# Gated cross-attention and experts on one core: diagonals of the maxima in halves, norms on ScalarE, a reordered second layer

## The reference

```
x = x + tanh(g_xattn[0]) * mha(layernorm(x), ctx)                 # 16 heads of 16, softmax over 128 keys
x = x + tanh(g_ffn[0])   * soft_experts(layernorm(x))             # 8 experts, silu(gate)*up, routing weights
x = x + tanh(g_xattn[1]) * attention(layernorm(x), ctx, mask)     # one head of 256
x = x + tanh(g_ffn[1])   * top1_experts(layernorm(x))             # 8 experts, relu, capacity 256 tokens each
```

## Time and profile before

| What | Value |
|---|---|
| median of 3 runs | 764.35 us (763.16 to 766.68) |
| profiled execution, its time | 764.7 us |
| its span, first to last instruction | 762.9 us |
| mean granted clock of TensorE | 0.921 of full speed |
| busy: TensorE, VectorE, ScalarE, GpSimd | 646.4, 521.0, 331.2, 229.1 us |
| transfers | 94.51 MB, mean 124 GB/s |

### The profile page before, as it was taken

The page is one execution under the profiler, slowest core; times in us unless marked ns, Lnnn a source line. Parts: engine busy times, 40 slices in busy tenths (PEclk is TensorE's granted clock), DMA queues, the critical chain, the costliest instruction groups (busy, mean ns, idle before and its releaser), DMA issues.

```text
span 762.9 us, 12648 instructions
## 1 busy us (share of the span) xinstructions
PE 646.4 (85%) x4564; PEld 546.7 (72%) x4564; DVE 521.0 (68%) x1362; ACT 331.2 (43%) x530; POOL 229.1 (30%) x155
## 2 busy tenths in 40 slices
PE   5978598899899899999799889999966931799995
PEld 4656366787678778778688777898855821799995
DVE  6877987677877866866776647479458883466662
ACT  4434155355356456456355325152523321455641
POOL 2444624566532212221014010010031242255542
PEclk9879779899999999999999999999989955799998
DMA  7303303335442242333243424434221141964700
GB/s 225 121 15 127 125 1 139 125 135 211 180 166 83 85 165 84 137 113 125 83 165 113 162 87 152 132 124 146 83 69 43 61 161 43 318 210 153 242 20 26
DMA packets 43463, 94.51 MB, mean 124 GB/s; under 512 B 3519, under 2 KB 24383, under 8 KB 42384
## 3 DMA queue, kind: packets, MB, share of 16 engines
q1 hardware_dynamic: 41344, 87.62, 33.6%
q0 software_dynamic: 2064, 6.16, 2.3%
HBM read 72.94 MB, written 21.04 MB: 123 GB/s over the span
## 4 chain that ended last, share of the span: by engine, by line
PE 65%; DVE 24%; issue 5%; ACT 2%; DMA 1%; POOL 1%; DVEq 0%; SPq 0%; ACTq 0%; POOLq 0%
PE psum L1591 43%; PE psum L2097 6%; PE psum L1668 2%; PE psum L1698 2%; PE psum L1628 2%; PE psum L1662 2%; DVE work L1063 1%; DVE scratch L266 1%; DVE x_all L1079 1%; PE psum L1635 1%; PE psum L1647 1%; DVE work L951 1%; PE psum L1962 1%; PE psum L1893 1%; PE psum L1945 1%
## 5 line engine op out<-in xcount | busy, mean ns | idle before, releaser
L1591 PE MATMUL psum<-arena 128*128 128x256 f32 (+1 forms) x2544 | 446.0, 334 | 33.8 <-DVE x_all L1079 15.6
L1591 PEld LDWEIGHTS psum<-arena 128*128 128x128 f32 x2544 | 384.5, 199 | 78.4 <-DVE x_all L1079 14.8
L2135 POOL TENSOR_TENSOR diag<-neg_ident,work 128x1024 fp32r<-128x1024 f32 x32 | 60.9, 1904 | 249.3 <-DVE work L1010 242.5
L1063 DVE TENSOR_TENSOR work<-work,psum 128x512 f32<-128x512 f32 x64 | 43.9, 686 | 62.1 <-PE psum L1591 57.3
L625 ACT ACTIVATE arena<-work 128x512 fp32r<-128x512 f32 x64 | 40.3, 630 | 90.7 <-DVE work L1063 78.7
L1079 DVE SCALAR_TENSOR_TENSOR x_all<-psum,w_exp,x_all 128x256 f32<-128x256 f32 x128 | 55.9, 479 | 27.7 <-PE psum L1591 26.9
L618 ACT ACTIVATE work<-psum 128x512 f32<-128x512 f32 x64 | 38.2, 597 | 56.8 <-PE psum L1591 56.3
L1068 DVE TENSOR_TENSOR arena<-work,arena 128x512 fp32r<-128x512 f32 x64 | 51.8, 810 | 8.7 <-ACT arena L625 8.2
L2218 POOL TENSOR_TENSOR arena<-work,arena 128x1024 fp32r<-128x1024 f32 x4 | 9.5, 2370 | 151.1 <-ACT arena L641 151.1
L1010 DVE TENSOR_REDUCE work<-psum 128x8 f32<-128x1024 f32 x32 | 39.0, 1220 | 15.7 <-PE psum L1647 15.6
L593 ACT ACTIVATE work<-psum 128x1024 f32<-128x1024 f32 x32 | 32.8, 1026 | 35.4 <-PE psum L1668 32.3
(11 more groups left out here) (194 smaller groups left out, 844.8 us busy)
## 6 DMA issues: line engine op xcount, KB each, us to landing
arena<-kept SPq DMA_DIRECT2D x24, 1024.0 KB, 5.6
work<-in_w SPq DMA_DIRECT2D x16, 1024.0 KB
kept<-arena SPq DMA_DIRECT2D x8, 1536.0 KB, 6.1
arena<-kept SPq DMA_DIRECT2D x24, 512.0 KB, 4.8
work<-in_w SPq DMA_DIRECT2D x8, 768.0 KB, 7.8
slots<-fill POOLq DMA_DIRECT2D x1, 2080.0 KB
work<-in_ctxT SPq DMA_DIRECT2D x8, 256.0 KB, 3.0
work<-in_ctxT SPq DMA_DIRECT2D x4, 512.0 KB, 5.2
```

The lines of the kernel that those rows point to most:

```text
L1063: dve.tensor_tensor(gu[i % 2], gu[i % 2], ps[:, UP, :], ALU.mult).then_inc(hm, 1)
L1591: mm = pe.matmul(dst, left(i, k), right(j, k), start=(n == 0), stop=(n == 3 * K2 - 1))
L2135: pool.tensor_tensor(diag, neg_ident[:, :].rearrange("p (o q) -> p o q", o=1).to_broadcast([P, 8, P]), mx[u % 2].rearrange("p (h o) -> p h ...
```

## The change

It has these parts.

- **Diagonals.** GpSimd writes the eight diagonals in two instructions of four heads, each with its own increment of `dg`; the first of the two products of `shift` waits for the first half only.
- **Routing weights.** `expert_weights` no longer divides the two best weights by their own sum, since all weights are divided by their sum afterwards; one clamp goes and the last two multiplies are one.
- **Norms of layer 1.** `normalise_a` and `normalise_b` are now Identity activations of ScalarE with a scale and a shift; VectorE writes the shift (one instruction) behind each root. `root_b` writes its root and shift where the row for the slots carries them, so that `row_numbers` goes.
- **Values.** The bias of the values is added to x by GpSimd (`value_bias`, 16 additions of 128x256) after the norm has read it; `v1_evict` is a copy by ScalarE.
- **Row numbers** come from constants for all groups; the count of a group's experts stands behind `dest`.
- **Order of turn3**, on all engines: group ga+1's moments and root stand first, its transposes and keys are made inside the turn, queries stand before values, and `scores1(ga)` before `xb_transpose(gb)`.
- **Filler products** (`keep_warm`): bf16 128x512 products into a bank that nobody reads, 2, 22, 5, 2 and 4 in the last turn, 5, 2 and 4 in the one before, 44 before the slots.
- **First expert of the slots**: both its low parts are made by VectorE (`first_split`), the second one after all dispatches have landed; GpSimd does no split before its last dispatches.
- **Slots.** The first load is of two tiles, then two, then twelve. All but the first pair of norms are made by ScalarE, after the fourth Relu of a half turn.
- **The end.** The last `down4` signals its first tile by itself and puts the second tile into the other bank; the addition and store of the first tile follow at once. `scatter` waits for each tile by itself.

```diff
 def expert_weights(g):
-    divide_by_sum(7)
     seq(dve.tensor_tensor(r[7], r[7], over_e(rs[1]), ALU.mult))
     seq(dve.tensor_tensor(rt[4], rt[4], rt[7], ALU.add))
-    divide_by_sum(4)
+    seq(dve.tensor_reduce(rs[2], r[4], AX.X, ALU.add))
+    seq(dve.reciprocal(rs[2], rs[2]))
...
-    dve.tensor_scalar(w_exp[g % 2], r[4], tgate[:, 2:3], None, ALU.mult).then_inc(s_wexp, 1)
+    dve.scalar_tensor_tensor(w_exp[g % 2], r[4], tgate[:, 2:3], over_e(rs[2]), ALU.mult, ALU.mult).then_inc(s_wexp, 1)
 def shift(u):
-    pe.wait_ge(dg, u + 1)
     for j in range(2):
+        pe.wait_ge(dg, 2 * u + j + 1)
         mm = pe.matmul(ps[:, ST + j, :], ones_r[:, :], diag[:, 4 * j:4 * j + 4, :], ...
 def diagonals(u):
...
-    pool.tensor_tensor(diag, neg_ident..., mx[u % 2]..., ALU.mult).then_inc(dg, 1)
+    for j in range(2):
+        sel = slice(4 * j, 4 * j + 4)
+        pool.tensor_tensor(diag[:, sel, :], neg_ident..., mx[u % 2][:, sel]..., ALU.mult).then_inc(dg, 1)
+def normalise_b(g):                                  # ScalarE; normalise_a alike
+    act.wait_ge(sb_ok, g + 1)
...
+        act.activation(xn_b[t % GB], x_all[:, t, 0:D], ACT.Identity, bias=x_all[:, t, D + 1:D + 2],
+                       scale=x_all[:, t, D:D + 1]).then_inc(nb, 1)
 def turn3(ga, gb):                                   # VectorE
+    if more:
+        stats_a(ga + 1, 0); moments_a(ga + 1, 0); root_a(ga + 1, 1)
     attention_gates(gb)
-    if ga is not None:
-        xa_low(ga)
     add_attention(gb)
     moments_b(gb)
-    root_b(); normalise_b(gb)
-    if ga is not None:
-        v1_add(ga)
-    row_numbers(gb)
-    xb_low(gb)
+    root_b(gb)
     if ga is not None:
         mask_and_max(ga)
-    if ga is not None and ga + 1 < G:
-        stats_a(ga + 1, 0); moments_a(ga + 1, 0); root_a(ga + 1, 1); normalise_a(ga + 1)
+    xb_low(gb)
+    if ga is None:
+        first_split(0, w4_l1.sem)
     pick_expert(gb)
-    count_experts(gb)
+    slot_and_gate(gb)
     pick_place(gb)
+    if more:
+        xa_low(ga + 1)
 def turn3(ga, gb):                                   # TensorE
     probs_transpose(gb)
-    if ga is not None:
-        xa_transpose(ga)
+    if last: keep_warm(2)
     attend(gb)
-    if ga is not None:
-        k1_project(ga); v1_project(ga); q1_project(ga)
+    if last: keep_warm(22)
+    else: q1_project(ga); v1_project(ga); scores1(ga)
     xb_transpose(gb)
-    if ga is not None:
-        scores1(ga)
+    if more: xa_transpose(ga + 1)
+    else: keep_warm(5)
     logits1(gb)
+    if not more: keep_warm(2)
     logits1_transpose(gb)
+    if more: k1_project(ga + 1)
+    else: keep_warm(4)
     places(gb)
+xa_transpose(2); k1_project(2)
 turn3(2, 1); turn3(3, 2); turn3(None, 3)
+keep_warm(44)
 def turn3(ga, gb):                                   # ScalarE
     probs_copy(gb)
     if ga is None:
-        split(0, 0, 0)
+        split(0, 0, 0); split(0, 0, 1)
     else:
-        xa_high(ga); k1_evict(ga); q1_evict(ga)
+        q1_evict(ga)
+        if more: normalise_a(ga + 1)
+        v1_evict(ga)
+    normalise_b(gb)
     xb_high(gb)
...
     gate_exp(gb)
+    if more: xa_high(ga + 1); k1_evict(ga + 1)
 # GpSimd, after the weights of layer 1
 ctx_low(0)
+value_bias(0); value_bias(1); ctx_low(1); value_bias(2)
 pool.wait_ge(s_disp, 16)
-ctx_low(1); ctx_low(2); dispatch(0); ctx_low(3); dispatch(1); dispatch(2); split_w1(0, 0); dispatch(3)
+ctx_low(2); dispatch(0); value_bias(3); ctx_low(3); dispatch(1); dispatch(2); dispatch(3)
 for f in range(8):                                   # ScalarE, turn of the slots' experts
     hidden(g, i, f)
     if more and f == 1:
         split(*nxt, 0)
+    if more and f == 3:
+        act.wait_ge(s_xs[1 + i], 16)
+        slots_norm(*nxt)
```

More of the change, by code:

```diff
@@ L335, in block_kernel @@
         oh1, loc1, dest = sem("onehot_ready"), sem("places_ready"), sem("rows_ready")
-        s_xs = [sem("first_slots_loaded"), sem("other_slots_loaded")]
+        s_xs = [sem(f"{n}_slots_loaded") for n in ("first", "second", "other")]
         s_raw4 = [sem(f"expert1_weights_loaded{i}") for i in range(2)]
@@ L634, in zone_exps, with normalise_a @@
                 act.activation(rt[5], rt[3], ACT.Exp, scale=-1.0 / 0.3).then_inc(r_out, 1)
+            def normalise_a(g):
+                act.wait_ge(sa, g + 1)
+                if g:
+                    act.wait_ge(nat, GB * g)
+                else:
+                    act.wait_ge(x1t, B)
+                for t in range(g * GB, (g + 1) * GB):
+                    act.activation(xn_a[t % GB], x_all[:, t, 0:D], ACT.Identity, bias=shiftA[:, t:t + 1], scale=rstdA[:, t:t + 1]
+                                   ).then_inc(na, 1)
             def ctx3_high(g):
@@ L841, in _ @@
             silu(31, 1)
+            normalise_a(2)
+            h_high(31, 1)
             ctx3_high(2)
-            h_high(31, 1)
             exponentials1(1)
             def turn3(ga, gb):
+                more = ga is not None and ga + 1 < G
                 probs_copy(gb)
@@ L880, in hidden, with slots_norm @@
                 act.activation(h4[i][0][:, f, :], ps[:, f % 4, 0:CAP], ACT.Relu).then_inc(h1_hi.sem, 1)
+            def slots_norm(g, i):
+                for j in range(2):
+                    row = xs[:, bass.ds(4 * g + 2 * i + j, 1), :].rearrange("p a c -> p (a c)") if not isinstance(g, int) \
+                        else xs[:, 4 * g + 2 * i + j, :]
+                    act.wait_ge(xd_t.sem, xd_t.now(g, 1) if i else xd_t.before(g, 2))
+                    act.activation(xd[j], row[:, 0:D], ACT.Identity, bias=row[:, D + 1:D + 2], scale=row[:, D:D + 1]
+                                   ).then_inc(xd_ok.sem, 1)
             def turn(g, last):
@@ L1161, in root_a @@
                                 newtonA[:, 0:groups * GB])
[L1163 to L1171, removed]
+                dve.scalar_tensor_tensor(shiftA[:, sel], mvA[:, sel, 0:1].rearrange("p n o -> p (n o)"), -1.0, rstdA[:, sel],
+                                         ALU.mult, ALU.mult).then_inc(sa, groups)
             weights_low(0)
@@ L1380, in xb_low @@
                                       ).then_inc(nb_lo, 1)
-            top, rank, gate, row, place, own = (r3s[i] for i in range(6))
+            top, rank, gate, row, place = (r3s[i] for i in range(5))
             def over8(col):
@@ L2091, in down4 @@
                 pe.wait_ge(y4.sem, y4.before(g, i + 1))
+                if last:
+                    pe.wait_ge(y4.sem, y4.now(g, 1))
                 for j in range(2):
+                    bank = 4 if last and j else 4 + i
                     for f in range(8):
@@ L2106, in turn @@
                         slots_transposed(*((g, 1) if i == 0 else (g + 1, 0)))
-                    down4(g, i)
+                    down4(g, i, last and i == 1)
             slots_transposed(0, 0)
```

235 lines of the change are left out of this document (134 added, 101 removed).

## The result

The changed kernel takes 740.6 us (median of 4 runs, 739.94 to 743.88) against 763.75 us (761.9 to 766.68): ratio 0.9702, 95% interval 0.9659 to 0.9745. Forecast was 742 us. Its profiled execution took 739.94 us, 24.76 less than that of before; the span is 738.1 us, the mean clock 0.965.

What follows compares the result with a forecast made beforehand. TensorE was taken to bound the mixed stage and the slots' experts, with gains only where it waits. 5.1 + 1.75 + 1.0 + 8.4 + 2.25 + 2.4 + 1.75 = 22.65 us off 764.7 gave 742 us, range 735 to 752.

Steps and rivals of the forecast that it cites:

- Routing weights: Mixed stage, four group changes: six VectorE instructions, 1.28 us a group, leave the chain TensorE waits for; 5.1 us gained.
- Diagonals: Mixed stage: the second half ends 0 to 0.74 us later, covered by TensorE's queue; 0, bounds -0.2 and +1 us.
- Other edits of the mixed stage: Value bias, normalisations, values' evictions, constants' columns: off TensorE's path; 0, bounds -2 and +2 us for ScalarE's in-order queue.
- Turn (2,1): Second attention layer: by the new order, group 2's attention starts at 592.5 instead of 594.25; 1.75 us gained.
- The port stall: GpSimd's additions hold VectorE through the shared port: turn (2,1) about 3 us poorer; as a rival 748 us, chance 0.08.
- Turn (3,2): Second attention layer: a chain of 18.2 us instead of 19.2 between two attentions; 1.0 us gained.
- Last turn: Attention(3) to row numbers: 8.4 us gained; port stall 4.2, clock kept by fillers 3.2, norms 0.6, row counting 0.4.
- Row numbers to slots: Between row numbers and first slots: dispatch 1.15, halved first load 0.5, faster first transposes 0.6; 2.25 us gained.
- First 48 products: Start of the slots' experts: 2.4 us gained if the 44 fillers keep the clock up until the slots are there.
- the clock rival: Last turn and slots' start: the clock falls anyway, so 6.2 us stay; 748.2 us, chance 0.22.
- Slots' stage, 0, and the end, 1.75: Slots' norms on ScalarE cost 0, bound +0.5 us for each of seven; earlier last stores gain 1.75 us.
- the rival of a late ScalarE: Norms, key evictions and splits in one queue, last turn and slots' stage: 8 us lost, 750 us, chance 0.12.

Runs made afterwards that it cites:

- norm_first: The changed kernel with ScalarE's normalisation of group 0 ahead of h_high(29, 1) instead of behind it: 737.14 us, ratio 0.9664 to the kernel before.
- after_whole_diag: The changed kernel with the diagonals written whole again, in one GpSimd instruction: 739.62 us, ratio 0.9702 to the kernel before.
- split_late: The kernel before with GpSimd's split of the slots' first expert moved behind its last dispatch, nothing else: 757.98 us, ratio 0.9931.
- after_no_filler: The changed kernel without any filler product: 743.85 us, ratio 0.9763 to the kernel before.
- more_filler: The changed kernel with 56 instead of 44 fillers before the slots and 9 between first transposes and first products: 739.63 us, ratio 0.9697.
- halves_only: The kernel before with the diagonals in two halves and nothing else: 761.35 us, ratio 0.9989.
- weights_only: The kernel before with the new routing weights and nothing else: 752.07 us, ratio 0.9873.

## Why the forecast held, step by step

- **Routing weights, 5.1 us: mis-sized, too low.** The instructions came off as said; the forecast priced the clock at nothing. Alone the edit measured 9.7 us. In the changed kernel's trace the four group changes gave 6.2 of the 9.4 us of layer 0. For the rest no single cause is shown; at the last group change the clock is.
- **Diagonals, 0: right.** The second half ends 0.2 us later and TensorE doesn't see it; two kernels say 0.
- **Other edits of the mixed stage, 0 (bounds -2 and +2): the mechanism named, the size wrong.** ScalarE's queue did stand ahead, but it was its norms (2.06 us for the four, 1.70 said) that were late behind a h_high, and the clock made more of it than its length: a wait of 1.37 us, a shift of the silus around it by 2.1, and 2.7 us regained in norm_first, of which 1.7 went again in later turns.
- **Turn (2,1), 1.75 us: mis-sized, 3.75.** The layout used the durations of before, and those belonged to a clock of 0.81 (the attention product of group 1 took 3.30 us, now 1.99); now the stretch runs at 1.00, and without any filler the turn is as long, 21.79 us. So it is the new order, and not the fillers, that goes with the higher clock; that it causes it was read from the traces, no run undid the order by itself, and in after_whole_diag, with the same order, the logits took 2.40 us at a clock of 0.65 and the turn 22.96 us. The port stall that the rival priced at up to 3 us measured 1.2.
- **Turn (3,2), 1.0: the number right, 1.25, by luck.** The term was a shorter chain in the new order. Without fillers the turn takes 19.66 us, 0.5 more than before the change; the fillers, which the forecast priced in the last turn alone, give 1.7.
- **Last turn, 8.4: 7.55.** Port 4.4 (4.2 said) and fillers 3.2 (3.2 said) were each shown alone. They fill the 7.55 by themselves, so nothing is left for the norms and the counting (1.0 said). These two were not measured alone, but split_late (old norms and counting) and after_no_filler (new ones), both without stall and without fillers, take 20.38 and 20.45 us to the row numbers' end.
- **Row numbers to slots, 2.25: right, 2.65.** The dispatches are 0.96 to 0.97 us, 1.15 less for the one.
- **First 48 products, 2.4: wrong, it lost 1.55.** The condition was named (the fillers keep the clock until the slots are there) and it failed: gaps of 2.22 and 1.90 us, clock 0.50 from 629 to 635. This is the clock rival, in its last term only. But the clock isn't what lost the term: in more_filler it stays up, and the next transposes are still bound to the raw weights. The step that failed is that these were taken to cost nothing (0, bound +2.5): ScalarE waited 2.50 us for them, and the second transposes come 22.78 us after the row numbers, 1.1 earlier than in the kernel before (23.89) and no earlier than in halves_only (22.72), which has the old code there. So of the 4.65 us of this term and the one above at most 1.1 arrived, and 1.55 of the 2.65 were handed back here. The 8.67 us that the term started from was besides a long one: the same 48 products took 7.63, 7.67 and 7.92 us in halves_only, split_late and weights_only.
- **Slots' stage, 0, and the end, 1.75: right.** From the second expert's transposes to the end it takes 100.8 us in the kernel before and the three kernels made from it, and 99.03 to 99.05 in all ten made from the changed one.

The total was nearer than its parts, and that is luck: 4.3 us in layer 0 and 2.0 in turn (2,1) on one side, 4.0 at the slots' start and 0.85 in the last turn on the other. Of the rival of a late ScalarE one part came true, the 2.5 us for the raw weights; its rest, a bound by ScalarE and no change fell with the stretches that they named.

## What to carry to other kernels

Price a TensorE wait with the clock after it, not only with its length: here 5.1 us of instructions were worth 9.7 (6.3 to 13.1), and 1.1 us of waiting moved the next milestone by 2.7. Durations laid out for a new order must be scaled to the clock that the new order will have. And look at what arrives next before a gap is filled or a load moved: 36 products made 2.6 us shorter gave nothing that can be shown, because the next step waited for a transfer. More fillers met the raw weights, earlier weights met the slots, and an addition moved out of one turn's root met the next one's.

## What was not expected of the hardware

- The clock's falls in one program differ from execution to execution: 50 to 60 us ran at 0.55, 0.56, 0.84, 0.98 and 1.00 in five kernels with nearly the same code there, and with it the events at 62 us stand 3 to 5 us earlier or not. The length of a turn repeats better: turn (2,1) took 21.79 to 21.85 us in six kernels with the same order, but 22.96 in a seventh, after_whole_diag.
- A fall needs no long wait: 1.37 us in a stretch that was busy 1.63 of 3 us was followed by 0.50.
- GpSimd holds VectorE instructions with one input too: TENSOR_SCALAR of 128x4 took 0.66 us instead of 0.17, while the aggregate beside it kept its 0.38. In halves_only a TENSOR_SCALAR of 128x4 took 3.74 us beside the split of the weights.
